# A two-layer graph network on one core: the second layer's product taken in the other order

## The reference, cut to what matters

```
# layer 0, 16 heads of 32
a  = q k^T * 512**-0.5 + 2*adj ; p = softmax(a)  (rows that are all zero give 0)
x1 = layernorm(x + (p v) Wo^T)
# layer 1, four experts
scores = x1.mean(axis=nodes) @ router_w + router_b ; top1 = argmax(scores)
out    = adj @ (x1 @ expert_w[top1])
y      = relu(batchnorm over all graphs of one expert(out))
result = layernorm(x1 + y)
```

## Time and profile before

| | us |
|---|---|
| time, median of 3 runs (2672.56 to 2677.76) | 2675.96 |
| the profiled execution's own time | 2680.46 |
| its span in the profile | 2678.7 |
| PE busy | 2336.3 (87%) |
| DVE busy | 2075.9 (77%) |
| POOL busy | 1784.4 (67%) |
| ACT busy | 1715.0 (64%) |
| one graph in the steady state, from sum- to the next sum- | 146.7 |

### The profile page before, as it was taken

The page is one execution under the profiler, slowest core; times in us unless marked ns, Lnnn a source line. Parts: engine busy times, 40 slices in busy tenths (PEclk is TensorE's granted clock), DMA queues, the critical chain, the costliest instruction groups (busy, mean ns, idle before and its releaser), DMA issues.

```text
span 2678.7 us, 50494 instructions
## 1 busy us (share of the span) xinstructions
PE 2336.3 (87%) x14976; PEld 1826.5 (68%) x14976; DVE 2075.9 (77%) x5107; ACT 1715.0 (64%) x3838; POOL 1784.4 (67%) x3148
## 2 busy tenths in 40 slices
PE   2678999999999999999999999999999999986433
PEld 2456777777777777777777777777777777765332
DVE  2687878887887878788888878787887887872588
ACT  0467676777767676767677676777776776762232
POOL 0678786877777777868777777777786877770000
PEclk7789898999989898989999898989998999987755
DMA  6577464555555565646555555656464555523597
GB/s 213 185 233 228 147 216 147 172 175 159 173 176 177 153 204 149 214 143 190 158 162 173 177 177 154 204 154 205 151 212 136 173 167 175 148 81 122 189 332 248
DMA packets 215897, 478.88 MB, mean 179 GB/s; under 512 B 41424, under 2 KB 49616, under 8 KB 208720
## 3 DMA queue, kind: packets, MB, share of 16 engines
q1 hardware_dynamic: 215632, 475.71, 56.7%
HBM read 274.23 MB, written 67.11 MB: 127 GB/s over the span
## 4 chain that ended last, share of the span: by engine, by line
PE 68%; DVE 13%; ACT 5%; issue 5%; POOL 4%; SPq 3%; DMA 2%; DVEq 0%; POOLq 0%; ACTq 0%
PE t_bank L334 14%; PE p_bank L252 12%; PE p_bank L254 11%; PE p_bank L253 11%; PE o_bank L347 9%; PE s_bank L325 7%; PE p_bank L288 3%; SPq L646 2%; DVE att L468 2%; ACT att L407 2%; POOL fold L617 2%; DVE ln_raw L1004 2%; DVE att L494 1%; POOL fold L619 1%; DVE xt L500 1%
## 5 line engine op out<-in xcount | busy, mean ns | idle before, releaser
L617 POOL TENSOR_TENSOR fold<-att 128x256 f32<-128x256 f32 x1024 | 821.3, 802 | 471.3 <-DVE nmax L468 366.9
L446 ACT ACTIVATE pt<-t_bank 128x512 f32<-128x512 f32 x1024 | 611.5, 597 | 561.1 <-PE t_bank L334 550.1
L468 DVE CUSTOM_DVE_ANT_0 att<-s_bank,adj_t 128x512 f32<-128x512 f32 x1024 | 699.0, 683 | 297.2 <-PE s_bank L325 295.4
L407 ACT ACTIVATE att<-att,nmax 128x512 f32<-128x512 f32 x1024 | 736.0, 719 | 85.5 <-POOL fold L617 63.2
L494 DVE TENSOR_SCALAR att<-att,small 128x512 f32<-128x512 f32 x1024 | 689.1, 673 | 9.3
L334 PE MATMUL t_bank<-ident,att 128*128 128x128 f32 x4096 | 644.4, 281 | 6.5 <-ACT pt L446 6.3
L334 PEld LDWEIGHTS t_bank<-ident,att 128*128 128x128 f32 x4096 | 515.7, 145 | 186.4 <-issue 48.5
L619 POOL TENSOR_TENSOR fold<-fold 128x128 f32<-128x128 f32 x1024 | 523.2, 511 | 80.3
L325 PE MATMUL s_bank<-k_stack,q_stack 128*128 128x512 f32 x1024 | 504.2, 493 | 80.4 <-DVE nmax L468 80.0
L624 POOL TENSOR_TENSOR fold<-fold 128x64 f32<-128x64 f32 x1024 | 357.9, 349 | 80.2
L347 PE MATMUL o_bank<-pt,v 128*32 128x256 f32 x4096 | 276.1, 415 | 28.0 <-ACT pt L446 15.6
(11 more groups left out here) (150 smaller groups left out, 3591.5 us busy)
## 6 DMA issues: line engine op xcount, KB each, us to landing
q_stack<-qk_t SPq DMA_DIRECT2D x1024, 64.0 KB, 2.0
k_stack<-qk_t SPq DMA_DIRECT2D x1024, 64.0 KB, 2.0
qk_w<-qk_split SPq DMA_DIRECT2D x123, 512.0 KB, 4.3
slot_a<-vo_split SPq DMA_DIRECT2D x16, 2048.0 KB, 8.2
slot_b<-vo_split SPq DMA_DIRECT2D x16, 2048.0 KB, 9.5
slot_a<-expert_split SPq DMA_DIRECT2D x16, 2048.0 KB, 8.1
stage<-in_xT SPq DMA_DIRECT2D x16, 1024.0 KB, 14.9
adj_t<-in_adj SPq DMA_DIRECT2D x64, 256.0 KB, 3.1
```

Source lines behind the costliest of these rows:

```text
L407: eng.activation(att[:, u % 4, j, :], att[:, u % 4, j, :], ACT.Exp, bias=nmax[:, u % 4, j:j + 1], scale=-1.0, accum_out=rsum[:, u % 4, j:j ...
L446: eng.activation(pt[:, j, :, (u % 2) * P:(u % 2 + 1) * P], t_bank[r % 2][:, :].rearrange("p (m n) -> p m n", m=NT), ACT.Copy).then_inc(act ...
L468: eng.tensor_tensor_reduce(out=att[:, u % 4, j, :], in0=s_bank[r % 2][:, :], in1=adj_t[:, t, :], scale=-2.0, scalar=3.0e38, op0=ALU.add, o ...
L617: eng.tensor_tensor(fold1[:, :], a[:, 0:256], a[:, 256:512], ALU.add).then_inc(pool_fold1, 1)
```

## The change

The second layer is computed as (adj x1) W in place of adj (x1 W). The first product now takes x1 with nodes on the partitions, as it lies, so the transposes X- are gone. S- is now x1^T adj^T (its low and high operands are x1 split in place, `x1t` high and `x1_lo` over `x1`), and M- is W^T times that, which has the layout that M- had before.

- The split of x1: ACT copies the high parts in u7 (one for each step), DVE writes the low parts in u9 j0 and j1, over x1, after the store of x1 has landed.
- The mean over the nodes: eight wide fp32r matmuls (ones by x1, high and low) in place of sixteen products with one column; the router's dot product is a DVE instruction on four partitions, and one small matmul spreads its four values.
- Buffers: Wv and the split adjacency are in `slot_b`, Wo and the expert in `slot_a`. S- waits for the adjacency's low parts, M- for the expert's load, which SP issues in u10 instead of u8.
- Batch-norm statistics are aggregated for each graph (`bn_aggr`, eight DVE operations for a graph instead of four).
- The order of the tasks: Q+0 begins in u6 j2 (before: u7 j0) and ends in u7 j1; K+0 is in u7 j1 to u8 j0; Q+1 in u8 j0 to j2 (before: u11 and u12); K+1 in u8 j3 to u9 j1 (before: u12 and u13); sum- in u9 j1 to j3; S- from u9 j3 to u12 j1, with route- in u10 j2 just ahead of S-1; M- from u12 j2 to u15 j0; Q+2 in u15.

```diff
 TASKS = [
     ("V", 0), ("V", 1), ("V", 2), ("V", 3),
     ("K", 2), ("O-", 0), ("O-", 1), ("Q", 3), ("O-", 2), ("K", 3),
     ("O-", 3),
-    ("Q+", 0), ("sum-", 0), ("route-", 0),
-    ("X-", 0), ("X-", 1), ("K+", 0),
-    ("S-", 0), ("X-", 2), ("S-", 1), ("X-", 3), ("S-", 2), ("S-", 3),
-    ("Q+", 1), ("M-", 0), ("K+", 1), ("M-", 1), ("M-", 2), ("Q+", 2), ("M-", 3),
+    ("Q+", 0), ("K+", 0), ("Q+", 1), ("K+", 1), ("sum-", 0), ("S-", 0), ("route-", 0),
+    ("S-", 1), ("S-", 2), ("S-", 3),
+    ("M-", 0), ("M-", 1), ("M-", 2), ("M-", 3), ("Q+", 2),
 ]
-COST = {"sum-": 0.4, "route-": 0.1, "X-": 0.2}
-HALF_SLOTS = [4, 4] * 2 + [3, 3] * 4 + [4, 0] + [4, 2] + [3, 2.6] + [3.3, 3.3] * 7
+COST = {"sum-": 0.7, "route-": 0.1}
+HALF_SLOTS = [4, 4] * 2 + [3, 3] * 4 + [4, 1] + [4, 2] + [3, 3] + [3.1, 3.1] * 7
...
             elif name == "sum-":
-                if c == 0:
-                    wait(eng, dve_x1, b, NT, 0)
-                for t in range(NT):
-                    mm = eng.matmul(bank[:, c:c + 1], x1[:, t, c * P:(c + 1) * P], ones[:, :],
-                                    start=(t == 0), stop=(t == NT - 1))
+                wait(eng, dve_lo["X"], b, NT, c + 1 - NT)
+                for part in (x1t, x1_lo):
+                    mm = eng.matmul(bank[:, :], ones_r[:, :].to_broadcast([P, P]), part[:, c, :],
+                                    start=(c == 0 and part is x1t), stop=(c == NT - 1 and part is x1_lo))
...
-            elif name == "X-":
-                mm = eng.transpose(bank[:, c * P:(c + 1) * P], x1[:, i, c * P:(c + 1) * P], ident[:, :])
             elif name == "S-":
-                if c == 0:
-                    wait(eng, dve_lo["X"], b, NT, i + 1 - NT)
-                    if i == 0:
-                        wait(eng, ld_ex, b, 16, 0)
-                mm = three_pass(eng, bank[:, :], lambda h: x1t[:, i % 2, h, c, :], lambda h: slot_a[:, h, c, :],
-                                c, c == DT - 1)
+                if c == 0 and i == 0:
+                    wait(eng, pool_at, b, NT, 0)
+                mm = three_pass(eng, bank[:, :], lambda h: (x1t, x1_lo)[h][:, c, i * P:(i + 1) * P],
+                                lambda h: slot_b[:, h, c, :], c, c == NT - 1)
             else:
                 if c == 0 and i == 0:
-                    wait(eng, dve_lo["S"], b, NT, 0)
-                    wait(eng, pool_at, b, NT, 0)
-                mm = three_pass(eng, bank[:, :], lambda h: sup[:, h, c, i * P:(i + 1) * P],
-                                lambda h: slot_b[:, h, c, :], c, c == NT - 1)
+                    wait(eng, dve_lo["S"], b, DT, 0)
+                    wait(eng, ld_ex, b, 16, 0)
+                mm = three_pass(eng, bank[:, :], lambda h: slot_a[:, h, c, i * P:(i + 1) * P],
+                                lambda h: sup[:, h, c, :], c, c == DT - 1)
...
+                if u == 7 and has_prev:
+                    wait(eng, dve_x1, b, NT, j + 1 - NT)
+                    wait(eng, pe["S"], b, DT, -DT)
+                    eng.activation(x1t[:, j, :], x1[:, j, :], ACT.Copy).then_inc(act_hi["X"], 1)
...
+                if u == 9 and j < 2 and has_prev:
+                    if j == 0:
+                        wait(eng, act_hi["X"], b, NT, 0)
+                        wait(eng, st_x1, b, 16, 0)
+                    for t in (2 * j, 2 * j + 1):
+                        dve_low(eng, x1_lo[:, t, :], x1[:, t, :], x1t[:, t, :]).then_inc(dve_lo["X"], 1)
...
-            if u == 8 and has_prev:
-                wait(eng, dve_pick, b, 3, -1)
-                if attends:
-                    wait(eng, pe["V"], b, NT, NT)
-                else:
-                    wait(eng, pe["S"], b, NT, -NT)
-                e = eng.value_load(pick[0:1, 0:1], min_val=0, max_val=E - 1)
-                eng.dma_start(slot_a[:].bitcast(F32),
-                              ex_dram[bass.ds(e, 1)].rearrange("a p h t n -> (a p) h t n")).then_inc(ld_ex, 16)
             if u == 8 and has_next:
                 stack(eng, b, 0, 4)
             if u == 9 and has_next:
                 load_qk_w(eng, b, 1, 5)
                 stack(eng, b, 1, 4)
+            if u == 10 and has_prev:
+                wait(eng, dve_pick, b, 3, -1)
+                wait(eng, pe["O"], b, NT, 0)
+                e = eng.value_load(pick[0:1, 0:1], min_val=0, max_val=E - 1)
+                eng.dma_start(slot_a[:].bitcast(F32),
+                              ex_dram[bass.ds(e, 1)].rearrange("a p h t n -> (a p) h t n")).then_inc(ld_ex, 16)
```

More of the change, by code:

```diff
@@ L33 @@
 NORM_UNITS = 2
+BN_OPS = 8
 TASKS = [
@@ L99, in build_gnn_layers @@
         adj_t = sb("adj_t", [P, NT, N])
-        x1 = sb("x1", [P, NT, D])
+        with nc.sbuf_tensor("x1", [P, NT, D], F32) as x1:
+            pass
+        x1_lo = sb("x1_lo", [P, NT, D], F32R)
         ot = sb("ot", [P, 2, GROUPS, N], F32R)
@@ L109, in build_gnn_layers @@
         bet = fold1[:, DT * E:2 * DT * E].rearrange("p (t e) -> p t e", t=DT)
-        bn_raw = sb("bn_raw", [P, B, DT, 6])
+        bn_mv = sb("bn_mv", [P, B, DT, 2])
         ident = sb("ident", [P, P])
         small = sb("small", [P, 64])
-        ones, eps_c = small[:, 0:1], small[:, 1:2]
+        ones_r = sb("ones_r", [P, 1], F32R)
+        eps_c = small[:, 1:2]
         rb, iota4 = small[:, 4:8], small[:, 8:12]
@@ L116, in build_gnn_layers @@
         ln_std, ln_rstd = small[:, 24:28], small[:, 28:32]
-        xmean = small[:, 32:36]
+        score = small[0:E, 32:33]
         rt = small[:, 40:56].rearrange("p (a e) -> p a e", a=4)
         ln_mv = small[:, 56:64].rearrange("p (t s) -> p t s", s=2)
-        rw = sb("rw", [P, DT, E])
+        rw = sb("rw", [E, D])
         nmax = sb("nmax", [P, 4, HG])
@@ L130, in build_gnn_layers @@
         o_bank = [pb("o_bank0"), pb("o_bank1")]
-        pe = {k: sem("pe_" + k) for k in ("score", "turn", "pv", "Q", "K", "V", "O", "sum", "route", "X", "S", "M")}
+        pe = {k: sem("pe_" + k) for k in ("score", "turn", "pv", "Q", "K", "V", "O", "sum", "route", "S", "M")}
         act_pt = sem("act_pt"); act_exp = sem("act_exp"); act_ot = sem("act_ot")
@@ L274, in pe_chunk @@
                 if c == 0 and i == 0:
-                    wait(eng, ld_wv, b, 16, 16)
+                    wait(eng, ld_wv, b, 16, 0)
+                    if b == 0:
+                        eng.wait_ge(dve_split, 6)
                 mm = three_pass(eng, bank[:, :], lambda h: xt[:, h, c, i * P:(i + 1) * P],
-                                lambda h: slot_a[:, h, c, :], c, c == DT - 1)
+                                lambda h: slot_b[:, h, c, :], c, c == DT - 1)
             elif name == "O-":
@@ L382, in act_task @@
                 eng.activation(v[:, i, :], bank[:, :], ACT.Copy).then_inc(act_v, 1)
[L383 to L387, removed]
             elif name == "S-":
@@ L523, in dve_task @@
                 wait(eng, pe["sum"], b, 1, 0)
-                eng.tensor_scalar(xmean[:, :], bank[:, 0:DT], 1.0 / N, None, ALU.mult).then_inc(dve_mean, 1)
+                eng.tensor_tensor_reduce(out=bank[0:E, :], in0=bank[0:E, :], in1=rw[:, :], scale=1.0 / N, scalar=0.0,
+                                         op0=ALU.mult, op1=ALU.add, accum_out=score).then_inc(dve_mean, 1)
             elif name == "route-":
@@ L535, in dve_task @@
                 eng.tensor_tensor(rt[:, 3, :], rt[:, 2, :], iota4[:, :], ALU.add).then_inc(dve_route, 1)
[L536 to L541, removed]
-                else:
-                    dve_low(eng, sup[:, 1, i, :], bank[:, :], sup[:, 0, i, :]).then_inc(dve_lo["S"], 1)
+            elif name == "S-":
+                wait(eng, act_hi["S"], b, DT, i + 1 - DT)
+                dve_low(eng, sup[:, 1, i, :], bank[:, :], sup[:, 0, i, :]).then_inc(dve_lo["S"], 1)
             elif name == "M-":
                 wait(eng, act_mixed, b, DT, i + 1 - DT)
-                row = slice(b - 1, b) if isinstance(b, int) else bass.ds(b - 1, 1)
-                eng.bn_stats(bn_raw[:, row, i, :].rearrange("p o s -> p (o s)"), x1[:, i, :]).then_inc(dve_bn, 1)
+                eng.bn_stats(ln_raw[:, i, :], x1[:, i, :]).then_inc(dve_bn, 1)
+                wait(eng, dve_bn, b, BN_OPS, 2 * i + 1 - BN_OPS)
+                eng.bn_aggr(bn_mv[:, b - 1, i, :], ln_raw[:, i, :]).then_inc(dve_bn, 1)
         def dve_choose(eng, b):
@@ L948, in _ @@
             dve.wait_ge(ld_const, 64)
[L949 removed]
+            dve.wait_ge(dve_bn, BN_OPS * B)
             dve.wait_ge(dve_choice, B)
             sums, squares = bn_s[:, 0], bn_s[:, 1]
[L952 to L961 removed]
+            mean, variance = bn_mv[:, :, :, 0], bn_mv[:, :, :, 1]
+            link(dve.tensor_scalar(sums, mean, float(N), None, ALU.mult))
+            link(dve.tensor_tensor(squares, mean, mean, ALU.mult))
+            link(dve.tensor_tensor(squares, squares, variance, ALU.add))
+            link(dve.tensor_scalar(squares, squares, float(N), None, ALU.mult))
             for e in range(E):
```

42 lines of the change are left out of this document (14 added, 28 removed).

## The result

The changed kernel takes 2978.61 us (median of 4 runs, 2976.18 to 2979.86) against 2674.26 for the kernel before: 1.1135 times as long, 95% interval 1.1116 to 1.1154. The forecast was 2988 with a range of 2900 to 3050. The profiled execution took 2976.18, 295.7 more than that of before.

What follows compares the result with a forecast made beforehand. Q and K stacks on SP's queue block ACT's write to `qk_t`, then DVE's logits and POOL's low parts delay S-0. + 22 us for 14 graphs, with the ends, gives + 312 on 2680.5: 2992, less 4.5, 2988; range 2900 to 3050.

Steps and rivals of the forecast that it cites:

- T: End of the scores of u8 j3, where SP's Q stack starts; forecast to come 5 us earlier than before.
- Q+0's start to T: PE's chunks, steps, v-product, half clock and ACT's lateness ahead of T: 20.5 us, where it was 25.7.
- K+1 starts: On PE, once K's weights, issued behind the Q stack, have landed: T + 15.
- ACT writes K+1: ACT's high part into `qk_t` waits until the K stack's last landing: T + 23.7.
- POOL done: After the logits of u9 j2 and j3, a fold and two adjacency low parts: T + 32.6.
- S-0 starts: PE's S-0 waits for POOL's low parts: T + 32.5, while PE's own way would be ready at T + 25.
- S-0 to the next graph's first turn: 24 steps, 36 chunks, four v-products, route-, restart at half clock and two bank waits: 54.8 us.
- more per graph: 87.3 us from T to the next first turn where 60.5 was, less 5 ahead of T: + 22 us.
- The chain: Q stack, K stack, ACT's copy, DVE's low part and logits, POOL's low parts, S-0: T + 32.5 in all.
- The two bank waits: PE waits at S-1 for S-0's bank, 1.0 us, and at M-0 for S-3's low part, 1.6 us.
- What the profile would show: ACT waiting some 10 us per stack; PE gaps of about 14 us before K+1 and 8 before S-0; 169 us a graph.
- The rest: Outside the 14 graphs' + 308: first graph + 20, last graph - 4, tail - 12; together + 312.

Runs made afterwards that it cites:

- take POOL's part out: The changed kernel with all four of POOL's low parts of the adjacency at the end of u8, none in u9: 2873.1 us.
- the order alone: The kernel before with only Q+1 and K+1 moved to right behind K+0: 2860.4 us, 1.0692 times.
- The run with K's weights first: The changed kernel with SP's load of K's weights moved from u9 to u8, ahead of the Q stack: 2968.8 us.
- Q+1 and K+1 late: The changed kernel with Q+1 and K+1 put back in their old places, u12 and u13, all else kept: 2768.6 us.
- the inputs moved forward: The 2769 us kernel (Q+1 and K+1 back late) with adjacency high and low parts and x1's low parts moved into u8: 2629.7 us, 0.9844 times the kernel before.
- the last placement: The 2667 us version (x1's low parts in u8 j1, j2) with POOL's four low parts two in j1, two in j2: 2598.0 us.

## Why the prediction was right

Point by point, by its own steps, for the graph shown; T is 2341.92.

| step | predicted | measured |
|---|---|---|
| Q+0's start to T | 20.5 | 20.4 |
| K+1 starts | T + 15 | T + 13.95 |
| ACT writes K+1 | T + 23.7 | T + 23.5 |
| POOL done | T + 32.6 | T + 31.9 |
| S-0 starts | T + 32.5 | T + 32.1 |
| S-0 to the next graph's first turn | 54.8 | 54.0 |
| more per graph | 22 | 20.5 |

- *Ahead of T.* The 12 chunks, nine steps, v-product, half clock and ACT's lateness came out. PE waited 1.11 us for ACT ahead of the v-product, for which 1.6 was taken.
- *The chain.* Its start and its end are right and were tested: take POOL's part out and 105 us go; put the order alone into the old kernel and it slows by 187. The middle is right only in part. The prediction let the K stack and ACT's copy decide when DVE gets free, put PE's own way at T + 25, well inside, and x1's low parts at nothing. In eleven of 15 graphs DVE does not wait for ACT's copy: it is held by PE's late scores (behind K's weights) and by x1's low parts (2.08 and 1.67 us). That the two branches end within 1.3 us of each other is why the forecast of T + 32.5 still holds; nothing in the prediction says that they should, so that much is luck. The run with K's weights first shows that the branch by the K stack alone gives nearly the same time.
- *What no run varied.* That the stacks are slow to issue, and when SP starts them, rests on the rows alone.
- *From S-0 on.* The two bank waits were 0.44 and 0.79 us, for which 1.0 and 1.6 were taken.
- *What the profile would show* was wrong in one place. It said that ACT would wait some 10 us for each stack. For the Q stack it does (11.8), but for the K stack 0.3 to 2.3, since K+1, held by its weights, ends only then. The prediction's own times gave this (K+1 finished near T + 21, the stack landed at T + 23.7) and the sentence did not follow them. The gap ahead of K+1 was forecast at about 14 us; it is 14.4 to 15.0 in the other graphs (15.8 in the first), and the one shown is the shortest.
- *The rest.* By the v-products of PE, the first graph costs 17.7 us more (20 was forecast), the next 14 together 288.9 (308), and from there to the end it is 10.9 less (16 less). The last of these is a sum of two misses. Up to O-'s wait for Wo the last graph took 6.5 us more where 4 less was forecast: POOL's wait was 8.03 us, and PE waited 1.54 and 2.32 us for x1's low parts, which the prediction left out. What comes behind took 17.4 less where 12 was forecast. In all the forecast was 312 above the profiled execution, and the measured difference is 296.
- *The rule on relieving the engine with the highest occupancy.* By occupancy the Trainium skill's "Perfetto Trace Analysis", Identifying the Most-Contended Engine, names PE here (87%), and PE's busy time did fall by 64 us while the kernel slowed by 296. The rule says where to look; it does not say that the work taken out stood on the path, nor what a changed order waits for.
- *The rule on issuing.* The Trainium skill's "DMA: Bandwidth & Descriptors", Issuing engines are not separate DMA queues, says that initiating a DMA is usually small beside the DMA. The rows agree for one DMA of 64 KB only so far: some 0.6 us beside 2.0 to the landing. But the issues stand in line: 16 took 10.0 us, and the last landed 2 us later, so for a stack as a whole the issue is the larger part.
- *What was not foreseen* is the kernel without the stacks. The expectation for Q+1 and K+1 late was 2600 and it was 2769; it priced PE's work and one wait for POOL (5 us; it was 6.67), and not x1's low parts, 4.05 us late, nor the clock lost behind the two gaps (granted 0.53 over 4.9 us behind the first, 0.52 over 4.8 behind the second). With the inputs moved forward it was 2630, and in the last placement 2598.

## What to carry to other kernels

Before a task is moved to an earlier place, follow its result: here the block was computed early, but the one buffer that it goes to was still being emptied by 16 DMAs that could not start sooner, and everything queued behind the blocked copy, on three engines, waited too. The longest gap by name (13.95 us, K's weights) was on the path in most graphs, and taking it out still gave only some 10 us of 296, because a second branch ended within 1.3 us of it. So look for what arrives just before the last arrival, and read more than one graph: the same program showed either branch. And when an order is changed, give each input's producer (the split, the low part) a new place with it: three placements of the same eight low parts, in the same order of tasks, lay between 2598 and 2667 us.

## What the runs showed of the hardware

- A busy TensorE can run at half clock. In the kernel before it fell to half in the gaps ahead of Q+0, came back, and fell again in sum-, sixteen products with one column each (32 records), though PE was busy 7.85 of 8.2 us (granted 0.62; 0.50 in the v-product behind it). With four wide fp32 matmuls in their place, and route- cut from 8 records to 2 in the same edit, it was 1.00 over the 15 us from 2010 to 2025, sum-, route- and the v-product among them, and the kernel gained 62 us.
- The same gap need not have the same effect. In the 2598 us version PE waits 2.33 us for a logit in each of two neighbouring graphs. In one it goes on at full clock (a score matmul at 1881.74 takes 0.47 us) and falls behind a later gap of 0.54; in the next it goes on at half (the same matmul at 2024.13 takes 0.77).
- One issue took some 0.6 us of SP's queue (10.01 us for the sixteen of the Q stack), so that 16 DMAs of 64 KB held it for 10.0 to 11.1 us, with 2.0 from an issue to its landing.
